# A two-layer graph network on one core: the sync engine fetches one tile in 48 of layer 0's gathered rows, by stored byte addresses

## The reference

```python
# layer 0
h = relu(edge_feat @ W1 + b1); w = (h @ W2 + b2).reshape(e, 4, MUL, MUL)
s_e, v_e = s[src], v[src]
m0 = ALPHA * (einsum('ei,eio->eo', s_e * sh0, w_000) + C110 * einsum('eim,em,eio->eo', v_e, sh1, w_110))
m1 = ALPHA * (einsum('ei,em,eio->eom', s_e, sh1, w_011) + einsum('eim,eio->eom', v_e * sh0, w_101))
x = layernorm(x + segment_sum(m, dst) + SI_SCALE * selfmix(x))
# layer 1
R = relu(edge_weight[:, None] @ w1 + b1) @ w2 + b2
Fj = x[src]; Y = spherical_harmonics(edge_attr_3)
x = layernorm(x + zeros.at[dst].add(messages(R, Y, Fj)))
```

## Time and profile before

| | us |
|---|---|
| median of 3 runs | 4051.86 |
| lowest and highest run | 4048.19 and 4052.96 |
| the profiled execution's own time | 4059.36 |
| its span, first to last instruction | 4057.4 |

### The profile page before, as it was taken

How to read it: one execution, slowest core, us unless ns; L and a number is a source line. 1 busy time by engine, 2 the same in 40 slices (tenths; PEclk the granted TensorE clock), 3 DMA queues, 4 the chain that set the end, 5 groups by cost and what they waited for, 6 DMA issues and landing times. The chain is left out here.

```text
span 4057.4 us, 95500 instructions
## 1 busy us (share of the span) xinstructions
PE 3377.3 (83%) x23156; PEld 1945.7 (48%) x23156; DVE 3460.9 (85%) x5277; ACT 2184.8 (54%) x6587; POOL 2953.0 (73%) x3087
## 2 busy tenths in 40 slices
PE   4777777777777777777559999999999999999996
PEld 3444444444444444444335555555555555555553
DVE  8888888888888888888759999889889888988887
ACT  3555555555555555555335565555555555555554
POOL 5777777777777777777377777777777777777772
PEclk7888888888888888888779999999999999999998
DMA  3111111111111111111212222222221222222221
GB/s 107 35 33 32 34 32 33 34 33 35 32 33 32 33 32 34 36 32 33 35 38 48 45 44 44 44 44 44 47 45 41 47 44 44 44 43 44 44 44 28
DMA packets 238827, 162.68 MB, mean 40 GB/s; under 512 B 143937, under 2 KB 212594, under 8 KB 238066
## 3 DMA queue, kind: packets, MB, share of 16 engines
q1 hardware_dynamic: 104338, 91.78, 8.7%
q0 software_dynamic: 98560, 50.66, 8.6%
q10 hardware_dynamic: 35650, 17.88, 1.7%
HBM read 148.83 MB, written 10.43 MB: 39 GB/s over the span
## 5 line engine op out<-in xcount | busy, mean ns | idle before, releaser
L430 POOL DMA_INDIRECT rows<-x_rows,src x1540 | 1483.2, 963 | 536.6 <-issue 526.6
L430 POOL DMA_INDIRECT rows<-in_x,src x1540 | 1468.9, 954 | 485.6 <-issue 472.3
L775 PE MATMUL red<-prod,ident 128*128 128x336 f32 (+1 forms) x4704 | 1511.2, 475 | 1.4 <-DVE prod L1073 1.2
L775 PEld LDWEIGHTS red<-prod,ident 128*128 128x128 f32 x4704 | 892.3, 195 | 635.4 <-issue 193.3
L1073 DVE TENSOR_TENSOR prod<-wps,arena 128x896 f32<-128x896 f32 x782 | 832.4, 1083 | 176.2 <-PE wps L762 159.0
L755 PE MATMUL wps<-bias_parts,ones 64*128 64x448 bf16 (+1 forms) x2346 | 471.4, 398 | 610.7 <-DVE prod L1067 452.4
L565 ACT ACTIVATE gap<-iota,slot_plan 128x128 bf16<-128x128 f32 x3136 | 935.6, 386 | 7.0
L762 PE MATMUL wps<-w_sb,hidden 64*128 64x448 f32 (+1 forms) x3920 | 746.9, 476 | 0.0
L583 ACT ACTIVATE arena<-red 128x336 f32<-128x336 f32 (+1 forms) x294 | 135.5, 461 | 1103.5 <-PE red L775 1102.9
L755 PEld LDWEIGHTS wps<-bias_parts,ones 64*128 64x128 bf16 x2346 | 114.6, 94 | 1135.3 <-DVE prod L1067 562.4
L1082 DVE TENSOR_REDUCE arena<-prod 128x384 f32<-128x3072 f32 (+1 forms) x195 | 520.9, 2671 | 0.1
(11 more groups left out here) (127 smaller groups left out, 3025.3 us busy)
## 6 DMA issues: line engine op xcount, KB each, us to landing
mlp<-in_dist SPq DMA_DIRECT2D x196, 256.0 KB
fetched<-in_x SPq DMA_DIRECT2D x3072, 0.1 KB
fetched<-x_rows SPq DMA_DIRECT2D x3072, 0.1 KB
mlp<-in_feat SPq DMA_DIRECT2D x98, 256.0 KB
rows<-in_x,src POOLq DMA_INDIRECT x1540
rows<-x_rows,src POOLq DMA_INDIRECT x1540
frames<-frame ACTq DMA_DIRECT2D x49, 144.0 KB
geo<-frames ACTq DMA_DIRECT2D x98, 72.0 KB
```

Source lines behind the costliest of these rows:

```text
L430: nc.gpsimd.indirect_dma_start(out=rows[z][:, t, :], out_offset=None, in_=table_rows, in_offset=bass.IndirectOffsetOnAxis(ap=src_sb[z][:, ...
L775: ins = nc.tensor.matmul(red[:, bank * 512:bank * 512 + cols], ident[:], pr[:, i, :, a:b, :], start=(i == 0), stop=(i == MUL - 1))
```

## The change

Constants and loads first. In layer 0 a group is now six chunks with two fetched tiles, one in every third chunk (chunks 2 and 5 of a group, slots 0 and 1), one tile in 48; its 128 rows are issued in parts of 43, 43 and 42 behind the three `load_mlp`. In layer 1 it stays at one tile in 64. There are now two buffers `fetched`, two `row_fetched` and a `tile_moved` per slot, for both of which SP raises counts in advance. A fetched tile is thus waited for in either slot.

The numbers that SP loads into registers aren't row numbers any more but byte addresses. They are made once at the start: SP loads all row numbers of the fetched tiles (`fetch_all`, 24 x 384), DVE shifts them left by 7, ACT stores them to DRAM (`fetch_offsets`), and SP waits for that before its loops. Source and target of a row fetch are then viewed as bytes (128 of `uint8`), and the register computation ahead of each fetch is gone. A register load takes up to 22 numbers in layer 0, and 16 as before in layer 1.

`src_sb` holds the row numbers of a whole group and has two buffers, used in turn by groups. SP loads the next group's at the last chunk of a group, in one transfer, and POOL waits for them at a group's first chunk alone. Both engines' loops now hold two groups.

In layer 1 the two DMAs of `load_mlp` have become one, whose source is an array of 2 x 64 x 1024 elements with step 0 in the middle, and whose target is all 128 partitions.

```diff
-FETCH_PARTS = (32, 32, 32, 32)
-FETCH_LOAD = 16
-FETCH_CHUNKS = len(FETCH_PARTS)
-FETCH_ROUNDS = FETCH_CHUNKS // RING
-FETCHES = ROUNDS // FETCH_ROUNDS
+FETCH_PARTS = ((43, 43, 42), (32, 32, 32, 32))
+FETCH_LOADS = (22, 16)
+FETCH_EVERY = tuple(len(parts) for parts in FETCH_PARTS)
+FETCH_CHUNKS = (6, 4)
+FETCH_TILES = tuple(chunks // every for chunks, every in zip(FETCH_CHUNKS, FETCH_EVERY))
+FETCH_ROUNDS = tuple(chunks // RING for chunks in FETCH_CHUNKS)
+FETCHES = tuple(ROUNDS // rounds for rounds in FETCH_ROUNDS)
+FETCH_PAIRS = tuple(fetches // 2 for fetches in FETCHES)
+FETCH_COLS = (slice(0, FETCH_TILES[0] * P), slice(FETCH_TILES[0] * P, sum(FETCH_TILES) * P))
+ROUNDS_AHEAD_OF_TILE = ((1, 2), (2, 1))
...
-MLP_LOADS = (1, 2)
+MLP_LOADS = (1, 1)
...
-        src_sb = slots(lambda z: sb(f"src{z}", [P, TILES], I32))
+        src_sb = slots(lambda b: sb(f"src{b}", [P, max(FETCH_CHUNKS) * TILES], I32))
...
-                self.src_loaded = ring("src_loaded", 16)
+                self.src_loaded = slots(lambda b: sem(f"l{n}_src_loaded{b}"))
...
+            sp.dma_start(fetch_all[:], src_fetched).then_inc(loaded["fetch"], 16)
...
-            def load_source(n, z, r, k):
-
-                s = layers[n]
-                sp.wait_ge(s.rows_read[z], r)
-                sp.dma_start(src_sb[z][:], src[bass.ds(k, 1)].rearrange("k p t -> p (k t)")
-                             ).then_inc(s.src_loaded[z], 16)
+            def load_source(n, b, group):
+
+                source = (src_0, src_1)[n]
+                sp.dma_start(src_sb[b][:, 0:FETCH_CHUNKS[n] * TILES], source[bass.ds(group, 1)].rearrange("g p t -> p (g t)")
+                             ).then_inc(layers[n].src_loaded[b], 16)
...
-                    for a in range(2):
-                        sp.dma_start(mlp_sb[z][a * HID:(a + 1) * HID, :],
-                                     dist[bass.ds(k, 1), a, :].broadcast_to([HID, CHUNK // 2])
-                                     ).then_inc(s.mlp_loaded[z], 16)
-
-            def fetch_rows(n, part):
-
-                table_rows = x if n == 0 else x1
-                p0 = sum(FETCH_PARTS[:part])
-                for p in range(p0, p0 + FETCH_PARTS[part], FETCH_LOAD):
-                    _, indices = nc.values_load_multi_w_load_instructions(
-                        fetch_index[0:1, p:p + FETCH_LOAD], engines=(mybir.EngineType.SP,), min_val=0, max_val=N_NODES - 1,
+                    sp.dma_start(mlp_sb[z][:], dist[bass.ds(k, 1)].rearrange("k a c -> (k a) c").unsqueeze(1)
+                                 .broadcast_to([2, HID, CHUNK // 2])).then_inc(s.mlp_loaded[z], 16)
+
+            def slot_of_tile(n, a):
+                return ((a + 1) * FETCH_EVERY[n] - 1) % RING
+
+            def fetch_rows(n, a, part):
+
+                rows_as_bytes = (x if n == 0 else x1).bitcast(U8).rearrange("r c -> (r c)")
+                row, z = FEAT * 4, slot_of_tile(n, a)
+                end = sum(FETCH_PARTS[n][:part + 1])
+                for p in range(end - FETCH_PARTS[n][part], end, FETCH_LOADS[n]):
+                    _, offsets = nc.values_load_multi_w_load_instructions(
+                        fetch_index[0:1, a * P + p:a * P + min(p + FETCH_LOADS[n], end)], engines=(mybir.EngineType.SP,),
+                        min_val=0, max_val=(N_NODES - 1) * row,
                         skip_runtime_bounds_check_because="the indices of the edges' sources are rows of the table")
-                    for a, index in enumerate(indices):
-                        sp.dma_start(fetched[p + a:p + a + 1, :], table_rows[bass.ds(index, 1), :]
-                                     ).then_inc(row_fetched, 16)
+                    for i, offset in enumerate(offsets):
+                        sp.dma_start(fetched[z][p + i:p + i + 1, :].bitcast(U8),
+                                     rows_as_bytes[bass.ds(offset, row)].unsqueeze(0)).then_inc(row_fetched[z], 16)
+
+            def move_tile(n, a, r):
+
+                s, z = layers[n], slot_of_tile(n, a)
+                sp.wait_ge(row_fetched[z], 16 * P)
+                sp.sem_clear(row_fetched[z])
+                sp.wait_ge(s.rows_read[z], r)
+                sp.wait_ge(s.rows_copied[z], r)
+                sp.dma_start(rows[z][:, TILES - 1, :], fetched[z][:]).then_inc(s.tile_moved[z], 16)
 
             def stream(n, count):
                 s = layers[n]
+                every, rounds = FETCH_EVERY[n], FETCH_ROUNDS[n]
                 with sp.Fori(0, count) as j:
-                    with sp.Fori(0, FETCHES) as h:
-                        f = sp.snap(j * FETCHES + h + 1 + n * (count * FETCHES))
-                        r0 = round_of(sp, j, h * FETCH_ROUNDS)
-                        sp.dma_start(fetch_index[:], src_fetched[bass.ds(h, 1), :]).then_inc(indices_loaded, 16)
-                        for m in range(FETCH_CHUNKS):
-                            z = m % RING
-                            r = round_of(sp, j, h * FETCH_ROUNDS + m // RING)
-                            k = h * FETCH_CHUNKS + m
-                            load_source(n, z, r, k)
-                            load_mlp(n, z, r, k)
+                    def group(h, b):
+
+                        f = sp.snap(j * FETCHES[n] + h + 1 + n * (count * FETCHES[0]))
+                        r0 = round_of(sp, j, h * rounds)
+                        sp.dma_start(fetch_index[:, 0:FETCH_TILES[n] * P], fetch_dram[bass.ds(h, 1), FETCH_COLS[n]]
+                                     ).then_inc(indices_loaded, 16)
+                        for m in range(FETCH_CHUNKS[n]):
+                            z, a = m % RING, m // every
+                            r = round_of(sp, j, h * rounds + m // RING)
+                            load_mlp(n, z, r, h * FETCH_CHUNKS[n] + m)
+                            if m == FETCH_CHUNKS[n] - 1:
+                                sp.wait_ge(s.rows_read[RING - 1], r0)
+                                load_source(n, 1 - b, h + 1)
                             if m == 0:
-                                sp.wait_ge(s.tile_moved, r0 * 16)
-                                sp.sem_inc(s.tile_moved, (FETCH_ROUNDS - 1) * 16)
+                                for c in range(RING):
+                                    sp.wait_ge(s.tile_moved[c], r0 * 16)
+                                    sp.sem_inc(s.tile_moved[c], ROUNDS_AHEAD_OF_TILE[n][c] * 16)
                                 sp.wait_ge(indices_loaded, f * 16)
                                 if n == 1:
                                     sp.wait_ge(x1_stored, len(PIECES) * 16)
                                 sp.sem_inc(fetch_turns, 1)
-                            fetch_rows(n, m)
-                        sp.wait_ge(row_fetched, 16 * P)
-                        sp.sem_clear(row_fetched)
-                        sp.wait_ge(s.rows_read[RING - 1], r)
-                        sp.wait_ge(s.rows_copied[RING - 1], r)
-                        sp.dma_start(rows[RING - 1][:, TILES - 1, :], fetched[:]).then_inc(s.tile_moved, 16)
-                    sp.wait_ge(s.tile_moved, round_of(sp, j, FETCHES * FETCH_ROUNDS) * 16)
-                    sp.sem_inc(s.tile_moved, 16)
+                            if a > 0 and m % every == 0:
+                                move_tile(n, a - 1, round_of(sp, j, h * rounds + (m - 1) // RING))
+                            if a > 0 and m % every == 1:
+                                sp.wait_ge(s.tile_moved[z], r * 16)
+                                sp.sem_inc(s.tile_moved[z], 16)
+                            fetch_rows(n, a, m % every)
+                        move_tile(n, FETCH_TILES[n] - 1, r)
+
+                    for z in range(RING):
+                        sp.wait_ge(s.rows_read[z], round_of(sp, j, 0))
+                    load_source(n, 0, 0)
+                    with sp.Fori(0, FETCH_PAIRS[n]) as pair:
+                        group(pair * 2, 0)
+                        group(pair * 2 + 1, 1)
                     for z in range(RING):
                         r = round_of(sp, j, ROUNDS - 1)
-                        load_source(n, z, r, (ROUNDS - 1) * RING + z)
+                        sp.wait_ge(s.tile_moved[z], r * 16)
+                        sp.sem_inc(s.tile_moved[z], 16)
                         load_mlp(n, z, r, (ROUNDS - 1) * RING + z)
 
+            sp.wait_ge(offsets_stored, 16)
...
-            def gather(n, z, r, tiles=TILES):
+            def gather(n, z, r, m, b, loads, tiles=TILES):
 
                 s = layers[n]
                 pool.wait_ge(s.rows_read[z], r)
                 pool.wait_ge(s.rows_copied[z], r)
-                pool.wait_ge(s.src_loaded[z], r * 16 + 16)
+                if m == 0:
+                    pool.wait_ge(s.src_loaded[b], loads * 16)
...
-                    with pool.Fori(0, FETCHES) as h:
-                        for m in range(FETCH_CHUNKS):
-                            gather(n, m % RING, round_of(pool, j, h * FETCH_ROUNDS + m // RING),
```

(21 more changed lines are left out.)

38 lines of the change are left out of this document (23 added, 15 removed).

## The result

The changed kernel takes **4402.0 us** (median of four runs, 4396.1 to 4404.2) against 4052.3 before: a ratio of **1.086**, 95% interval 1.085 to 1.088. The forecast was 4040 us with a range of 4030 to 4066. The direction, the size and the range are wrong.

A forecast was written before the change was run, and what follows sets the result against it. POOL's gathers were taken as the bound, one per 1.256 us in layer 0. Eight gathers fewer (-10.0), shorter waits (-2.5) and the start (+0.4) made -12.1 us; against the median of 4051.9 that gave 4040 us, range 4030 to 4066.

The forecast's parts named there:

- The register loads: SP, layer 0: six loads of 20 to 22 numbers per tile instead of eight of 16 save 0.9 us.
- the 117.0 us of the sum: SP's forecast work per layer 0 group of six chunks: 106.6 us for two tiles plus 10.4 for the rest.
- SP keeps up: Layer 0: SP needs 117.0 us per group against POOL's 118.1, 1.1 to spare; nothing is late up to 118.8.
- 11 of lead: At the start SP is 11 us ahead of POOL, which it can lose over 16 groups.
- 6 that DVE makes up: Some 6 us of SP's lateness that DVE recovers in the two chunks without a fetched tile.
- the first rival: SP is too slow, seen at the tile's move; at 15 ns more per row 26 us late, 4066 us; chance 0.13.
- The distances clog two engines: Rival: the one transfer fills two engines; hidden unless packets take more, at 20% more 157 us, 4197 us; chance 0.06.
- Eight gathers: Layer 0: POOL issues 8 gathers fewer at 1.256 us each, 10.0 us off, if SP keeps up.
- POOL's waits: POOL's waits for row numbers shrink with the numbers there in advance: 2.5 us off, between 0 and 5.6.
- The start: DVE's shift of the 24 x 384 numbers ahead of the loops: +0.4 us, between 0 and 2.
- Loops: Loops with two groups, taken with the single distances transfer: nothing, between -3 and +3 us.
- The gain is eaten up: Rival: PE in layer 1, DVE in layer 0 or a late SP loses 4 to 10 us: 4048 us; chance 0.20.

The follow-up runs named there:

- the mended kernels: Changed kernel with register loads starting on 16 bytes (parts 44, 44, 40) and distances in two transfers, ratio 0.9975, or in one from 16 rows, 0.9971.

## Why the prediction was wrong, point by point

**The register loads: the step that failed.** The prediction priced a load by its count: "51 ns for each number and 415 ns fixed; six loads of 20 to 22 instead of eight of 16 save 2 x 0.415 and two gaps, 0.9 us". Both ends of that line, one number and 16 numbers, came from loads that begin on a border, because parts of 32 in loads of 16 never leave it. Parts of 43 do, and nothing in the prediction asks where a load begins. The twelve loads of a group cost 12 x 1.50 = 18.0 us in the sum; they took 8 x 4.6 + 2 x 1.47 + 1.80 + 2.07 = 43.6 us. That is what carries SP from the 117.0 us of the sum to the 138.6 measured: 25.6 us more for the loads, 3.6 less for 256 rows (0.321 us each, where the sum had 0.335), 139.0 together. The line was wrong on the border too: 20 numbers take 1.46 us and 24 take 1.60, as it has them within 0.05, but 22 take 1.79, where it has 1.54.

The Trainium skill, "Runtime: NRT & Kernel Launch", section "Instruction fetch mechanics", has about 200 ns for each register that such a load fetches, "even for bulk". The loads off a border agree (0.2 us a number); those on a border don't, with 1.23 us for 16. An estimate by this figure of the Trainium skill gives the twelve loads 256 x 0.2 = 51 us, with SP as the bound; but it also gives 3.2 us to the loads of the kernel before, which take 1.23.

**SP keeps up: wrong, though the reckoning from SP's lateness to the time held.** The prediction's threshold was 118.8 us per group. SP took 138.6. By the prediction's own way of reckoning, 16 x (138.6 - 118.1) = 328 us less 11 of lead and 6 that DVE makes up are 311 us; over the forecast's 4040 that is 4351, and with layer 1's 43 to 47 us it is 4394 to 4398. Measured 4402. So the first rival had the place, the chain of waits but for POOL's row numbers, and the arithmetic; its price was 15 ns for a row, and that was wrong. Rows aren't what cost: at 0.321 us they are better than forecast, FUSED_REGOPS is gone and MOVE stays. The range's end of 4066 stood on the row's price alone; no end was given to the loads', though 22 numbers at an odd place were as little in the trace as a fetch by bytes was.

**The distances clog two engines: right on the mechanism, wrong on the place and both sizes.** The prediction gave it 0.06, let the load land in 15 us hidden behind ACT's spare time, and said that nothing happens until an engine is full. The load occupies two engines for about 11 us: a packet takes 170 ns on average there instead of 236, so that 128 of them are 22 us of engine time and not the 33 of that sum, which were all of SP's queue. And it is hidden from ACT in the middle of the layer. But others stand behind it: POOL's pause every 126 gathers grows by 2 to 5 us, 12 times. The prediction read POOL's gap of 0.30 us as the same everywhere; the 0.93 us at 2356.78 was in the trace. That the long pauses come from the two engines is shown, since they vanish with two transfers and with sixteen rows. What POOL waits for in a pause isn't: that older gathers must first have left some queue, and so the slowest engine decides, is an inference that would fit the lengths in layer 1, but no row names it, and it doesn't say why two pauses in three are missing in layer 0 of the mended kernels.

The rule of the Trainium skill that the prediction told ("DMA: Bandwidth & Descriptors", "Why a DMA increments its semaphore by 16 and not by 1"), on the engines that share a transfer, agrees with the trace at both ends: 1.9 engines for a source of 2 rows, and 13.8 for one of 16 rows.

**Eight gathers, -10.0 us, and POOL's waits, -2.5: the sum is right by luck, its parts aren't.** With both losses mended the change gives -0.25% to -0.29%, 10 to 12 us, where 12.1 were forecast, and 4040.6 us where 4040 were (0.9971 of 4052.1). But the waits for row numbers, though they went, brought nothing that shows: byte addresses, grouped row numbers and loops alone cost 12.7 us (4063.5 against 4050.8). One tile in 48 is worth some 23 us on top of them, as 1.0031 less 0.9971 to 0.9975 is 0.0056 to 0.0060, more than twice its price of 10.0. That the two errors cancel is chance. The range for the grouped row numbers (0 to 5.6 us off) had no loss in it.

**The start** is +0.4 us, as forecast (26.75 instead of 26.35 for POOL's first gather). **Loops** of two groups aren't what made layer 1 late; whether they have a part in the 12.7 us is open. **The gain is eaten up**: not by PE in layer 1, which let another 11 us through.

**The step between the layers**, +12.2 us, is part of the first loss: it is 55.5 us with aligned loads and 69 us with the distances alone mended.

## What to carry to other kernels

Price a register load by where it starts, not by its count alone: keep starts at multiples of four numbers (here 1.1 to 2.1 us against 3.4 to 4.7), and when parts are cut into new sizes, list the start of each load. An operation's price read from a trace holds for the shapes and starts that the trace has; a change from 32 to 43 leaves them, and the range has to say so. When two transfers are made one, look at the outermost dimension of the source, and ask not only who waits for the transfer but who stands behind it on the engines that it fills. And when a total comes out as forecast, test its parts: here one missed by 15 us and the other by 13, against each other.

## What the runs showed of the hardware

- Registers loaded from 16-byte borders: 16 numbers 1.14 to 1.23 us in most places (up to 1.7), 20 numbers 1.46, 24 numbers 1.60, 21 numbers 1.69, 22 numbers 1.79. Off a border: 16 numbers 3.46, 21 numbers 4.53, 22 numbers 4.67. With 21 numbers an offset of 4 bytes costs what 8 do, and with 22 numbers 8 cost what 12 do.
- A row's fetch with its address from a register: 0.321 us with the stored byte address (29 ns MOVE, 228 ns DMA), 0.411 us with the row number.
- One load of 128 packets of 4 KB: about 11 us from a source of 2 rows, 2.4 us from one of 16 rows, 2.7 us as two transfers.
- POOL's gathers pause every 126 of them (every eight chunks): by 0.4 to 1.0 us as a rule and up to 2.8, but by 3.3 to 5.8 us with few exceptions where two engines are busy for 11 us in every 20.
- On some chips a kernel that takes 4,050 us elsewhere takes 6,770, at a granted clock of 0.74 to 0.76, and in the stretch looked at SP's instructions mostly start 0.7 or 1.4 us apart or several together.
